# A four-layer Perceiver on one core: a third value buffer, no row maximum under a cap, work moved to GpSimd in the self-attentions, and eight PSUM banks for one layer's experts

## The reference

```python
# layer 0 self-attention (16 heads of 16): rotation of q and k, causal mask
scores = q @ k.T / sqrt(16); scores = where(causal, scores, -inf)
out = softmax(scores) @ v

# layer 2 self-attention (16 query heads, 4 key/value heads), CAP = 50
scores = CAP * tanh((q @ k.T / sqrt(16)) / CAP)
out = softmax(where(causal, scores, -inf)) @ v

# layer 3 self-attention: no softmax
resonance = sigmoid((align - 0.29514) * 15.0)
out = (resonance * gate_q[..., :, None] * gate_k[..., None, :]) @ v

# layer 2 feed-forward: one of 8 experts per token, each a 256 x 256 matrix
out = best_gate * (x @ expert_w[best])
```

## Time and profile before

| | |
|---|---|
| time, median of 3 executions | 2022.7 us (2019.74 to 2023.64) |
| the profiled execution, its own time | 2023.79 us |
| its span from the first to the last instruction | 2022.0 us |
| TensorE busy | 1821.4 us (90%) |
| VectorE, ScalarE, GpSimd busy | 1083.4, 815.1, 546.6 us |
| layer 0's self-attention | 183.8 to 252.9 us |
| layer 2's self-attention | 1380.8 to 1460.2 us |
| layer 2's feed-forward | 1460.2 to 1543.7 us |
| layer 3's self-attention | 1791.0 to 1875.2 us |

### The profile page before, as it was taken

The page is one execution under the profiler, slowest core; times in us unless marked ns, Lnnn a source line. Parts: engine busy times, 40 slices in busy tenths (PEclk is TensorE's granted clock), DMA queues, the critical chain, the costliest instruction groups (busy, mean ns, idle before and its releaser), DMA issues. The chain is left out here.

```text
span 2022.0 us, 42986 instructions
## 1 busy us (share of the span) xinstructions
PE 1821.4 (90%) x16746; PEld 1409.5 (70%) x16746; DVE 1083.4 (54%) x2711; ACT 815.1 (40%) x2356; POOL 546.6 (27%) x598
## 2 busy tenths in 40 slices
PE   8999779999999888899999799996688899996887
PEld 6886569745777746799999667775444577664786
DVE  7887841451466348675555445557733655355411
ACT  6663521131366243233333245552501566525231
POOL 4441213100244113201121023331202466412241
PEclk9999779999999999999999899998788999997898
DMA  4210069560243000143989331111102355200396
GB/s 142 59 50 4 3 237 319 169 206 31 66 102 101 16 41 3 52 173 131 332 331 333 131 131 49 49 33 43 40 15 68 104 156 157 64 1 2 120 341 224
DMA packets 86882, 233.93 MB, mean 116 GB/s; under 512 B 9648, under 2 KB 45008, under 8 KB 80176
## 3 DMA queue, kind: packets, MB, share of 16 engines
q1 hardware_dynamic: 81040, 216.01, 31.9%
q0 software_dynamic: 5664, 15.47, 2.4%
HBM read 216.23 MB, written 12.07 MB: 113 GB/s over the span
## 5 line engine op out<-in xcount | busy, mean ns | idle before, releaser
L2166 POOL TENSOR_TENSOR l1x_probs<-l1x_probs,l1x_total 128x512 f32<-128x512 f32 x64 | 65.1, 1038 | 209.5 <-DVE l1x_total L2391 209.5
L1487 PE MATMUL PS<-weights,l0x_ctxT 128*128 128x256 f32 x512 | 121.6, 388 | 0.0
L1034 PE MATMUL PS<-l1f_xT,l1f_slot 128*128 128x128 f32 x1024 | 117.0, 275 | 0.0
L1034 PEld LDWEIGHTS PS<-l1f_xT,l1f_slot 128*128 128x128 f32 x1024 | 115.7, 192 | 0.1
L1487 PEld LDWEIGHTS PS<-weights,l0x_ctxT 128*128 128x128 f32 x512 | 94.6, 191 | 15.4 <-issue 2.7
L2898 POOL TENSOR_TENSOR l2x_probs<-l2x_probs,l2x_total 128x512 f32<-128x512 f32 x64 | 65.1, 1038 | 137.2 <-DVE l2x_total L3072 137.2
L235 ACT ACTIVATE std<-moments,eps 128x8 f32<-128x8 f32 x13 | 3.9, 301 | 220.5 <-DVEq L173 135.3
L81 PE MATMUL PS<-consts 128*128 128x256 f32 x276 | 73.9, 423 | 16.1 <-PEq L87 16.1
L81 PEld LDWEIGHTS PS<-consts 128*128 128x128 f32 x276 | 57.8, 214 | 28.7 <-issue 19.9
L1155 DVE SCALAR_TENSOR_TENSOR l1f_product<-PS,l1f_slot,l1f_side 128x128 f32<-128x128 f32 x128 | 36.0, 344 | 65.9 <-ACT l1f_side L1111 65.9
L3362 PE MATMUL PS<-l3x_keysT,l3x_QW 128*128 128x289 f32 x256 | 67.7, 407 | 1.7 <-issue 1.7
(11 more groups left out here) (659 smaller groups left out, 4652.6 us busy)
## 6 DMA issues: line engine op xcount, KB each, us to landing
l1f_slot<-in_experts_up_dram SPq DMA_DIRECT2D x16, 2056.0 KB, 10.3
weights<-in_experts_up_dram SPq DMA_DIRECT2D x8, 2056.0 KB, 10.6
weights<-in_experts_down_dram SPq DMA_DIRECT2D x21, 640.0 KB, 5.8
weights<-in_experts_up_dram SPq DMA_DIRECT2D x10, 1024.0 KB, 7.8
l1f_slot<-in_experts_down_dram SPq DMA_DIRECT2D x16, 640.0 KB, 5.2
l0x_ctxT<-in_ctxT_dram SPq DMA_DIRECT2D x32, 257.0 KB, 2.6
l1x_ctxT<-in_ctxT_dram SPq DMA_DIRECT2D x32, 257.0 KB, 3.0
l2x_ctxT<-in_ctxT_dram SPq DMA_DIRECT2D x32, 257.0 KB, 2.6
```

Source lines behind the costliest of these rows:

```text
L1034: done = nc.tensor.matmul(PS[:, bank + a, m * P:(m + 1) * P], mat[:, c, m * P:(m + 1) * P], x, start=(c == 0), stop=(c == 1))
L1487: last = nc.tensor.matmul(PS[:, 2 * (b % 2) + k, half * D:(half + 1) * D], ctxT[b % SLOTS][:, c, half * P:(half + 1) * P], kw[:, c, k * D: ...
L2166: nc.gpsimd.tensor_tensor(p, p, bcast(total[b % 2][:, 2 * n:2 * n + 2], 2, KEYS), ALU.mult).then_inc(probs_done, 1)
```

## The change

1. A third buffer of value blocks in all three self-attentions: `blocks[t % 3]`, and the wait for an earlier product is for tile t - 3 in place of t - 2.
2. In "capped" and "resonance" the fourth of a tile's value blocks is written by GpSimd (`last_block`), with a semaphore of its own for which `weigh` also waits. GpSimd issues it for tile 0 ahead of the loop and for tile t + 1 behind its work for tile t.
3. In "capped" the maximum and its subtraction are gone (scores are at most 50), and the mask is no longer added ahead of the exponential but multiplied, as zeros and ones, behind it, by GpSimd instead of VectorE.
4. In layer 2's experts tile t uses bank t; the second half of the banks is released once the router's scores have been copied; the four unread matmuls wait until tiles 4 and 5 of the last round are summed, since they write bank 5.

```diff
-        self.blocks = two("blocks", [P, 16, TB, 17])
+        self.blocks = [sb(f"blocks{i}", [P, 16, TB, 17]) for i in range(3)]
+        self.shared_blocks = kind != "softmax"
...
+    def block_of(self, t, b):
+        to = self.blocks[t % 3][:, :, b, 0:16]
+        return to if self.kv_heads == 16 else to.rearrange("p (k r) d -> p k r d", k=self.kv_heads)
...
             pe.wait_ge(self.blocks_done, t + 1)
+            if self.shared_blocks:
+                pe.wait_ge(self.last_block_done, t + 1)
...
-            if t >= 2:
-                act.wait_ge(self.out_done, t - 1)
-            for b in range(TB):
...
+            if t >= 3:
+                act.wait_ge(self.out_done, t - 2)
+            for b in range(TB - 1 if self.shared_blocks else TB):
+                done = nc.scalar.activation(self.block_of(t, b), self.values(t), ACT.Copy, scale=batch_of[:, b:b + 1])
...
-            act.wait_ge(self.shifted, t + 1)
+            act.wait_ge(self.scores_read if self.kind == "capped" else self.shifted, t + 1)
...
+        def last_block(t):
+            pool.wait_ge(self.v_copied if gated is None else gated, t + 1)
+            if t >= 3:
+                pool.wait_ge(self.out_done, t - 2)
+            nc.gpsimd.tensor_scalar(self.block_of(t, TB - 1), self.values(t), batch_of[:, TB - 1:TB], None, ALU.mult).then_inc(self.last_block_done, 1)
+
+        if self.shared_blocks:
+            last_block(0)
         for t in range(NT):
...
+            else:
+                pool.wait_ge(self.exps_done if self.kind == "capped" else self.scores_read, t + 1)
+                p = self.probs[t % 2][:]
+                by = bcast(allowed, 1, 16) if self.kind == "capped" else bcast(factor[:, t, :], 2, S)
+                nc.gpsimd.tensor_tensor(p, p, by, ALU.mult).then_inc(self.probs_done, 1)
+            if self.shared_blocks and t + 1 < NT:
+                last_block(t + 1)
...
-        softmax = self.kind != "resonance"
+        softmax = self.kind == "softmax"
         ready = self.exps_done if softmax else self.probs_done
...
-                        last = nc.tensor.matmul(PS[:, t % 4, :], core.HT[:, c, t * P:(t + 1) * P],
+                        last = nc.tensor.matmul(PS[:, t, :], core.HT[:, c, t * P:(t + 1) * P],
...
+            pe.wait_ge(summed, (E // 2) * NT + 6)
             core.keep_busy(5, 4)
...
+            dve.sem_inc(summed, 4)
             first_best(core, dve, scores, number, best, place, gate)
```

More of the change, by code:

```diff
@@ L433, in values @@
         return rows if self.kv_heads == 16 else bcast(rows, 2, 16 // self.kv_heads)
+    def block_of(self, t, b):
+        to = self.blocks[t % 3][:, :, b, 0:16]
+        return to if self.kv_heads == 16 else to.rearrange("p (k r) d -> p k r d", k=self.kv_heads)
     def set_ones(self, pool, batch_of):
-        for i in range(2):
+        for i in range(3):
             last = self.core.nc.gpsimd.tensor_copy(self.blocks[i][:, :, :, 16], bcast(batch_of, 1, 16))
@@ L481, in weigh @@
                     last = nc.tensor.matmul(out[32 * g:32 * (g + 1)], self.probsT[t % 2][:, 4 * n + g, :],
-                                            self.blocks[t % 2][:, 4 * n + g].rearrange("p b d -> p (b d)"), start=True, stop=True)
+                                            self.blocks[t % 3][:, 4 * n + g].rearrange("p b d -> p (b d)"), start=True, stop=True)
             last.then_inc(self.out_done, 1)
@@ L621, in attend_vector @@
         for t in range(NT + 3):
-            if softmax:
-                if t < NT:
-                    mask(t)
-                if 0 <= t - 2 < NT:
-                    invert(t - 2)
-                if t < NT:
-                    tops(t)
-                if 0 <= t - 2 < NT:
-                    normalise(t - 2)
+            if softmax and t < NT:
+                mask(t)
+            if self.kind != "resonance" and 0 <= t - 2 < NT:
+                invert(t - 2)
+            if softmax and t < NT:
+                tops(t)
+            if self.kind != "resonance" and 0 <= t - 2 < NT:
+                normalise(t - 2)
             if 1 <= t <= NT:
@@ L1957, in _ @@
             rotation.gpsimd(pool)
-            at.attend_gpsimd(pool)
+            at.attend_gpsimd(pool, batch_of)
         @block.scalar
@@ L3121, in l2_self @@
     wqk, wv, wo = w.take(C, HEADS * 16), w.take(C, KV_HEADS * 16), w.take(C, D)
-    cos, sin, causal, side_of, batch_of = w.take(8), w.take(8), w.take(2 * S), w.take(2), w.take(TB)
+    cos, sin, allowed, side_of, batch_of = w.take(8), w.take(8), w.take(S), w.take(2), w.take(TB)
     cap = 50.0
@@ L3249, in _ @@
                         dve.wait_ge(expert_done, i * NT + (t + 1))
-                        bank = PS[:, t % 4, :].rearrange("p (e d) -> p e d", e=2)
+                        bank = PS[:, t, :].rearrange("p (e d) -> p e d", e=2)
                         step = nc.vector.scalar_tensor_tensor(core.X[:, t, :], bank[:, 0, :], gate[:, t, bass.ds(2 * i, 1)], core.X[:, t, :], ALU.mult, ALU.add)
```

48 lines of the change are left out of this document (17 added, 31 removed).

## The result

The changed kernel takes 1997.3 us (median of 4 executions, 1996.4 to 1999.3); the kernel before, on the same chip, 2021.45 (2019.7 to 2023.6). The ratio is 0.9882, 95% interval 0.9865 to 0.9899: 23.9 us less, between 20.4 and 27.3. The profiled execution took 1997.09 us, span 1995.0.

The account below looks back on a forecast made before the run. TensorE plus hand-overs bounded layer 2's experts, a buffer ring layer 3's self-attention, TensorE then VectorE layer 2's. Savings 10.0 + 8.8 + 1.5 = 20.3 us gave 2003.5 or 2002.4, stated as 2003.0; range 1998.5 to 2010.0.

Parts of the forecast that it names:

- Experts, -10.0: Layer 2's experts: eight banks remove seven hand-overs of 1.6 us, -11.1, less 1.1 at the end: net -10.0 us.
- the tail: End of layer 2's experts: unread matmuls wait for two second passes; if the barrier waits for them, 1.1 us.
- Layer 3's self-attention, -8.8: Layer 3's self-attention: three buffers unbind the ring and TensorE becomes the bound; -9.8 us, 1.0 given back: -8.8.
- The walk: Layer 3's self-attention, followed tile by tile: last weigh's last matmul at 1859.8 in place of 1869.6, -9.8 us.
- Layer 2's self-attention, -1.5: Layer 2's self-attention: tiles at 2.83 us, a later start and VectorE's additions to `x` counted: -1.5 us.
- The 0.4 for VectorE's additions: Layer 2's self-attention: VectorE's additions to `x`, between every second pair, cost 0.4 us, turning -1.9 into -1.5.
- (a): Layers 2 and 3 self-attention: TensorE's clock stays lower for most of both loops; 7.7 us less, 2016; chance 0.14.
- (b): Layers 2 and 3 self-attention: the last block on GpSimd takes 2 us, +7.5, 2010.5; chance 0.08.
- (d): Both self-attention loops: a last block so slow that GpSimd sets every tile; slower than before, e.g. 2033; chance 0.02.
- (c): Layer 2's experts: the loop still stalls at each jump back and at the end, leaving 5 of 10; 2008.5; chance 0.08.
- (e): Self-attention loops: clock rises after 5 us and no port loss; 1999 us; chance 0.10.
- the 1.1 for the port: Start of layer 2's self-attention: GpSimd's last block holds back VectorE operations on the shared SBUF port, +1.1 us.

Follow-up runs that it names:

- changed, four banks: The changed kernel with the four banks of layer 2's experts put back: 2007.6 us, 0.993 of the kernel before.
- third buffer alone: The kernel before with only the third value buffer added, ScalarE writing all four blocks: 2011.0 us, ratio 0.9953.

## Why the prediction was right in direction and 5.7 us short

The forecast was 2022.7 - 19.7; measured is 2021.45 - 24.1. The difference of 5.7 is made of four pieces: 1.3 because before itself came out lower; 0.6 by which I rounded up from my own 2002.4; 2.5 by which the three terms were too small; and 1.3 that none of the three blocks holds.

*Experts, -10.0.* The mechanism was right: from first to last product the loop went from 68.8 to 57.9 us, 10.95 less (forecast 11.1), and the tail costs 1.07 (forecast 1.1). The block's -10.9 has 1.0 more ahead of the loop: the router's 32 matmuls took 6.21 us before and 4.22 now, the same instructions at another granted clock. That isn't the change's: with four banks the router took 4.30 in "changed, four banks" and 4.25 in "third buffer alone". The term was still too small: the four blocks with four banks measured 82.8 to 83.5, the eight with eight banks and the delayed matmuls 71.6 to 73.2, 11.0 less in the mean, of which the loop has 11.4, less the tail of 1.07, and the stretch ahead of it 0.7.

*Layer 3's self-attention, -8.8.* The mechanism was right and the mis-sized part is "for hand-overs that aren't perfect and a rise that may be later I give back 1.0". The walk had the last weigh 68.3 us after the block's start, and it starts 68.4 after it (1844.06 - 1775.64). That the computed -9.8 meets the measured -9.7 is partly luck, for errors in it cancel: the clock rose 1.0 later than the walk had it and TensorE stopped for 0.74 without a cause in the trace, while the first weigh came 0.7 earlier (50.3 us into the block, forecast 51.0) and not one but two of the last steps have no compare. Most of the 0.7 is not the loop's: the first compare came 0.6 earlier, since 6 to 10 us into the block the granted clock was 0.57 before and 1.00 now. In the ten profiles with three buffers the block took 73.8 to 77.9, in the mean 9.3 less than the 84.2 with two buffers and all value blocks on ScalarE, so about half of the 1.0 would have been right. The clock rose 7.9 to 14.4 us after the first compare in them, and the latest rise goes with the longest block. That the third buffer does it all by itself, without GpSimd, was shown by adding it alone.

*Layer 2's self-attention, -1.5.* Here a step was wrong: "seven such VectorE operations stand on the way to the first compare: they wait 1.16 minus what little they get in first, +1.1". The row that I took it from the earlier trace rows had a GpSimd operation with two tensor inputs; the last block has one tensor and a scalar for each partition. It costs 0.20, and giving it a second tensor input brings the hold back. So the first weigh came 1430.31 - 1381.16 = 49.15 us into the block, 0.2 later than before (1429.7 - 1380.8 = 48.9) and not 0.9. The 0.4 for VectorE's additions didn't come on top either. Against both stands the multiplication, 1.27 and not 1.05: the tile took 2.93 and not 2.83, 0.5 more over five of them. The row for that price was the wrong one, a subtraction whose operand is repeated along the inner dimension. The Trainium skill (GPSIMD Engine Reference, Specifications) has the two engines collide where VectorE reads two SBUF inputs; the traces show that what it costs depends on GpSimd's operation as well. That the mask had better leave VectorE was right: its rule that elementwise work belongs there (Performance versus the Vector engine) is true of the operation, 0.68 against 1.27, and not of this loop, where following it costs 0.35 a tile (3.28 against 2.93).

*Layer 0's self-attention, 0*: 69.1 to 69.0, and 69.7 with the buffer alone, inside the 68.3 to 70.3 of all profiles.

*The rivals.* (a), a clock that stays low: in layer 3 it rose 57.0 us into the block in place of 56. The profile with all value blocks on ScalarE shows its beginning: a rise 5.9 us later after the first compare cost 2.1. (b) and (d) fell with 0.94 for the last block and 2.0 to 2.2 for GpSimd in a tile. (c) fell with the row of 128 matmuls. (e), a rise after 5 us and no port loss, came nearest in time, by its second half alone: the loss was 0.20 instead of 1.1, the rise came after 7.8.

*The range* was the other failed step: "The range reaches from (e), 1998.5". Its low end doesn't follow from rows: without the 1.1 for the port and with a rise 1 us earlier in two loops (1 - 2.46 / 4.1 = 0.4 each) the forecast comes to 2001, not 1999. And it was built from mechanisms of the touched blocks alone. The table shows what it left out: with nothing changed in them, layer 3's cross-attention comes out at 244.7 to 245.0 or 247.2 to 247.5, layer 1's feed-forward at 322.8 to 325.6, layer 3's at 141.5 to 148.4. Between the two profiles that the sum compares, the blocks outside the three differ by 4.2 (27.0 of span less 22.8). The third buffer alone has l3x at 244.7 with four banks, and eight banks alone have it at 247.3, so it isn't something that the change brings. A range of 3 us more at the low end would have held the time.

Whether the remaining 1.3 us belong to the change at all stays open; they lie inside the interval, and the same kernel run again saved 22.2 us, 0.6 less than the three blocks give.

## What to carry to other kernels

Where a loop hands buffers back and forth between two engines, price the ring and the engine that is busiest without it: one more buffer or four more banks gave here, to within 1 us over all profiles, the difference between the two, and engine time moved elsewhere (the fourth value block) gave nothing that could be measured. What can go wrong without a row to show it belongs into the range, not into the sum, together with what blocks that nobody touched wander by from one execution to the next. Price an operation by a row with the same layout of its operands. Move an operation by the chain and the queue it lands in, not by its own speed: the mask was faster on VectorE and the loop slower.

## What the runs showed of the hardware

- A GpSimd operation with two tensor inputs in SBUF held back a two-input VectorE operation until 0.14 us after its end (seen once, with the value block; behind the sines, which that operation reads, it is the same 0.14); one with a tensor and a per-partition scalar, 1.09 us long, cost VectorE 0.20 us over some five operations, the same in eight profiles.
- GpSimd takes 1.27 us for a 128 x 512 multiplication whose second operand changes from element to element, whether it is read sixteen times or laid out in full, and 1.05 where the operand is repeated along the inner dimension. The 128 x 256 block took 0.94 us as a tensor by scalar, and 0.66 as tensor by tensor with such a repeated operand.
- With the same loop in layer 3's self-attention, the granted clock of TensorE rose 8.5 us after the first compare in one profile and 14.4 in another, and the loop was 2.1 us longer. In blocks that nobody touched it differs as well: 0.81 or 0.62 over the same 18 us of layer 1's feed-forward, which took 322.8 or 325.4 us.
- In the gapless stretches of that loop TensorE stopped once or twice for 0.3 to 0.8 us within a row of matmuls, and the profile shows nothing that it waits for (0.74 in the changed kernel; 0.35 and 0.80 when it was run again). The cause was not looked for.
